# Delta-rule scan: the keys' products stored as five contiguous planes, and two moves in the first overlapped stage

## The reference

```
def step(Sm, inp):                       # one token; Sm is 8 x 8 for each head
    qi, ki, vi, bi = inp
    Sk = einsum('bhkv,bhk->bhv', Sm, ki)
    upd = ki[..., :, None] * (vi - Sk)[..., None, :]
    Sm = Sm + bi[..., None, None] * upd
    oi = einsum('bhkv,bhk->bhv', Sm, qi)
    return (Sm, oi)
...
h = hidden_states + o @ Wo
y = rmsnorm(h, ln2)
h = h + silu(y @ Wg) * (y @ Wu) @ Wd
...
h = silu(x @ w1 * s1) * (x @ w2 * s2)    # then two gelu layers 512 -> 512, and w3
```

## Time and profile before

| | |
|---|---|
| median of 3 runs | 1350.47 us (1347.79 to 1351.57) |
| profiled execution, its own time | 1351.84 us |
| its span (first to last instruction) | 1349.7 us |
| PE busy | 1164.6 us, 86% of the span |
| DVE busy | 910.4 us, 67% |
| ACT busy | 643.7 us, 48% |
| POOL busy | 473.0 us, 35% |

### The profile page before, as it was taken

The page is one execution under the profiler, slowest core; times in us unless marked ns, Lnnn a source line. Parts: engine busy times, 40 slices in busy tenths (PEclk is TensorE's granted clock), DMA queues, the critical chain, the costliest instruction groups (busy, mean ns, idle before and its releaser), DMA issues.

```text
span 1349.7 us, 19203 instructions
## 1 busy us (share of the span) xinstructions
PE 1164.6 (86%) x6118; PEld 616.3 (46%) x6118; DVE 910.4 (67%) x2097; ACT 643.7 (48%) x1258; POOL 473.0 (35%) x594
## 2 busy tenths in 40 slices
PE   5989889999898999999989581158899999999997
PEld 3434346454463554535535340124355455455553
DVE  3536535556577678686765776898888988988231
ACT  2061753745737537356365330314446745745642
POOL 3031220311323233143323136245356456466410
PEclk8989998999999999999989895578899999999999
DMA  3212030130311423314111239320220220200000
GB/s 100 83 48 71 1 110 9 46 98 34 110 41 29 139 64 81 94 33 143 39 44 42 58 70 239 97 50 9 49 58 16 58 57 16 57 24 8 24 9 8
DMA packets 85747, 79.83 MB, mean 59 GB/s; under 512 B 42800, under 2 KB 63408, under 8 KB 83632
## 3 DMA queue, kind: packets, MB, share of 16 engines
q1 hardware_dynamic: 85680, 79.01, 21.7%
HBM read 43.17 MB, written 35.00 MB: 58 GB/s over the span
## 4 chain that ended last, share of the span: by engine, by line
PE 60%; DVE 17%; ACT 10%; issue 7%; POOL 3%; DMA 2%; SPq 1%; ACTq 0%; DVEq 0%; POOLq 0%
PE ps L1318 14%; PE ps L1299 7%; PE ps L965 5%; PE ps L934 4%; PE ps L1002 4%; ACT arena L1451 4%; ACT arena L1413 3%; PE ps L968 3%; DVE arena L1850 3%; PE ps L975 3%; PE ps L1309 3%; PE ps L991 2%; PE ps L1069 2%; PE ps L1061 2%; PE ps L1051 2%
## 5 line engine op out<-in xcount | busy, mean ns | idle before, releaser
L1850 DVE TENSOR_REDUCE arena<-ps 128x4 f32<-128x512 f32 (+2 forms) x192 | 197.7, 1043 | 90.3 <-PE ps L968 87.4
L1318 PE MATMUL ps<-arena,late 128*128 128x512 f32 x512 | 227.0, 595 | 0.3 <-ACT arena L1600 0.3
L1413 ACT ACTIVATE arena<-ps 128x512 f32<-128x512 f32 (+2 forms) x200 | 109.7, 566 | 232.1 <-PE ps L934 105.6
L756 POOL TENSOR_SCALAR_AFFINE_SELECT arena<-arena 128x512 f32<-128x512 f32 x128 | 83.8, 657 | 295.1 <-ACT arena L1451 293.8
L1451 ACT ACTIVATE arena<-ps 128x1024 f32<-128x1024 f32 (+3 forms) x256 | 169.8, 711 | 33.3 <-PE ps L991 32.0
L1318 PEld LDWEIGHTS ps<-arena,late 128*128 128x128 f32 x512 | 96.3, 192 | 114.3 <-issue 112.0
L975 PE MATMUL ps<-mask_qk,ident_b 128*128 128x512 bf16 x450 | 124.2, 391 | 27.3 <-DVE arena L2134 26.1
L1600 ACT ACTIVATE arena<-ps,f_s 128x512 f32<-128x512 f32 x128 | 83.3, 688 | 109.4 <-PE ps L1318 98.5
L1413 ACT ACTIVATE arena<-ps,arena 128x128 f32<-128x128 f32 (+1 forms) x128 | 62.3, 529 | 125.1 <-DVE arena L1877 51.9
L934 PE MATMUL ps<-ident,arena 128*128 128x128 f32 (+1 forms) x624 | 99.2, 291 | 22.8 <-ACT arena L1413 13.1
L1299 PE MATMUL ps<-arena,late 128*128 128x512 f32 x256 | 115.6, 604 | 2.1 <-ACT arena L1600 2.1
(11 more groups left out here) (187 smaller groups left out, 1969.2 us busy)
## 6 DMA issues: line engine op xcount, KB each, us to landing
qr<-q_rep SPq DMA_DIRECT2D x8, 1024.0 KB, 5.6
kr<-k_rep SPq DMA_DIRECT2D x8, 1024.0 KB, 8.0
scan_d<-late SPq DMA_DIRECT2D x56, 138.0 KB, 3.0
arena<-scan_d SPq DMA_DIRECT2D x12, 552.0 KB, 6.8
q_rep<-hilo SPq DMA_DIRECT2D x24, 256.0 KB, 3.3
k_rep<-hilo SPq DMA_DIRECT2D x24, 256.0 KB, 3.9
proj_d<-arena SPq DMA_DIRECT2D x8, 768.0 KB, 5.1
late<-proj_d SPq DMA_DIRECT2D x8, 768.0 KB, 4.5
```

The costliest lines, as they stand in the source:

```text
L756: g.affine_select(out=block, in_=block, compare_op=ALU.is_ge, fill=0.0, base=0, pattern=[[0, 4], [1, P]], channel_multiplier=-1).then_inc( ...
L1318: last = pe.matmul(ps[:, ring2.bank(f"{n}{c}"), :], w[:, k, c * P:(c + 1) * P], src[:, k, :], start=(k == 0), stop=(k == HC - 1))
L1413: return act.activation(dst, src(ps[:, bank, :]), func, **kw)
L1850: v.tensor_reduce(heads[:, 2 * pr:2 * pr + 2, gs[0]:gs[-1] + 1], ps[:, at:at + 2, 0:len(gs) * w].rearrange("p q (n w) -> p q n w", w=w), X ...
```

## The change

1. `k_u` becomes five contiguous planes for each chunk, `[(chunk, j)][v][d]`: four planes of products and the old state as fifth. `live` is then a plane of 64 contiguous floats. The product writes 256 contiguous floats, reads the updates with a step of 4 floats in v (each held for 8 elements), and reads the keys with d innermost, a step of 256 bytes. The sum reads its five addends with a step of 64 floats (256 bytes), and writes 64 contiguous floats.
2. On POOL, in step 1 alone, the output products of tile 1's last quarter stand ahead of the gate products 0 and 1 of tile 0.
3. `AT_X` goes from 58 to 54: in step 1 `norm_x3` of tile 0 comes four scan instructions earlier.

```diff
-        k_u = [c2.take(QUARTER * HD, HD, CH + 1) for _ in range(2)]
-        live = [tile[:, :, :, CH].rearrange("p (c v) d -> p c v d", v=HD) for tile in k_u]
+        k_u = [c2.take(QUARTER * (CH + 1), HD, HD) for _ in range(2)]
+        live = [tile.rearrange("p (c j) v d -> p c j v d", j=CH + 1)[:, :, CH] for tile in k_u]
...
                     out_products(scan, h, 2, ahead is not None)
+                    out_products(scan, h, 3, True)
                     if ahead is not None:
                         gate_ab(ahead, 0)
                         gate_ab(ahead, 1)
-                    out_products(scan, h, 3, True)
...
-                    yield o.mark(v.tensor_tensor(k_u[half][:, rows, :, 0:CH], now_u.unsqueeze(2).broadcast_to([P, HD, HD, CH]),
-                                                 kt[:, c, :, :].unsqueeze(1).broadcast_to([P, HD, HD, CH]), ALU.mult))
+                    first = at * (CH + 1)
+                    yield o.mark(v.tensor_tensor(k_u[half][:, first:first + CH, :, :],
+                                                 now_u.rearrange("p v j -> p j v").unsqueeze(3).broadcast_to([P, CH, HD, HD]),
+                                                 kt[:, c, :, :].rearrange("p d j -> p j d").unsqueeze(2)
+                                                 .broadcast_to([P, CH, HD, HD]), ALU.mult))
...
-                    yield o.mark(v.tensor_reduce(after[:, (c + 1) % QUARTER, :, :], k_u[half][:, rows, :, :], X, ALU.add))
+                    yield o.mark(v.tensor_reduce(after[:, (c + 1) % QUARTER, :, :],
+                                                 k_u[half][:, first:first + CH + 1, :, :].rearrange("p j v d -> p v d j"), X, ALU.add))
...
-AT_Y, AT_H_FIRST, AT_H, AT_X, AT_S, AT_FIRST = 4, 21, 26, 58, 60, 44
+AT_Y, AT_H_FIRST, AT_H, AT_X, AT_S, AT_FIRST = 4, 21, 26, 54, 60, 44
```

## The result

| | median us | lowest to highest | runs |
|---|---|---|---|
| before | 1350.55 | 1345.19 to 1357.42 | 22 |
| changed | 1356.55 | 1349.88 to 1360.45 | 22 |

The ratio is 1.0041, 95% interval 1.0028 to 1.0055. Faster, at 1343.2 us, was forecast; the time lies in the stated range of 1340 to 1359, which the third rival (both far reads pay) had stretched, but on the wrong side of no change. Launches in a slower state are left out of every ratio: two of the kernel before in experiments 7 and 8, one of the changed kernel in 7, and one of 2782.51 us in experiment 6.

The account below looks back on a forecast made before the run. DVE's scan was taken to bound the start up to project_o at 953.18, PE the later steps. Terms -5.3 - 0.8 - 1.2 = -7.3 us gave 1343.2 us from 1350.47; range 1340 to 1359.

Parts of the forecast that it names:

- third rival: DVE scan: product and sum both pay fully for far reads, chunk +0.245 us, DVE becomes the bound, 1363.8 us; chance 0.27.
- Term 1: DVE's L2114: state read becomes contiguous instead of a 20-byte step, -196 ns a chunk (bounds -196 and 0).
- second rival: DVE's L2114 and ACT's L1658: state's read was not the cause, both stay slow, 1349.2 us; chance 0.06.
- Term 2: DVE's product reads keys at a 256-byte step, eight places: +20 ns a chunk (bounds 0 and +196).
- Term 3: DVE's sum reads five places 256 bytes apart: +25 ns a chunk (bounds 0 and +245).
- Term 4: ACT's copy of the states, L1658, becomes contiguous: 0.25 us off its 667 ns.
- later steps: PE's wait for ACT's takes of n2, n3 shrinks 0.25 us in five steps: -1.2 us (bounds 0 and -2.6).
- The start: From scan start to norm_x3 of tile 0: shorter chunks and AT_X bring it to 919.4 from 924.70, -5.3 us.
- GpSimd's order: Last quarter's output products ahead of the gates: 0.6 us, plus 0.2 from ACT's shorter copy, -0.8 us.
- tie: Gate product 0 comes later before layer m; the delay just fits into PE's idle 4.22 us ahead of project_o.
- The bound of 0.14 us a chunk: DVE's 2.17 us wait per step over 16 chunks: growth a chunk may take before DVE sets the step.

Follow-up runs that it names:

- experiments 7 and 8: 7: changed kernel again, 1.0026, and layout alone, 1.0058; 8: changed kernel, keys stored by token, gate product 0 ahead of output products again, 0.9965; all against before.
- experiment 6: Changed kernel with the keys of a tile stored by token, so the product reads 8 d in a row: 0.9965 to before, median 1346.28 us.
- experiment 1: Kernel before with 31 kinds of DVE instructions appended behind its last step, each twice, into scratch; single instructions timed, no kernel ratio given.
- experiments 3 and 4: Old layout: 3, GpSimd's new order plus AT_X at 54, 0.997; 4, the order alone, 0.9994, and AT_X at 54 alone, 0.9973; all against before.
- the second trace: Another trace of the unaltered changed kernel, ratio 1.0026 in that series: layer m 7.13 us, turn_h of tile 1 at 110.92 us against 110.95.
- the second series: Changed kernel timed once more beside the layout alone on one chip: 1.0026 (0.9993 to 1.006) to the kernel before.
- experiment 4's first: Kernel before with GpSimd's new order alone, AT_X at 58: 0.9994 (0.9972 to 1.0017).
- 7's first: Changed kernel run once more, unaltered, against the kernel before: 1.0026 (0.9993 to 1.006).

## Why the prediction was wrong

The step that failed is the choice between L1971 and L2114 as the nearest row for terms 2 and 3, "by the same row". Most of what stands around it held:

- **Term 1**, the state's read at -196 ns: -199. The second rival, another cause, is out (experiment 1, the held read).
- **Term 2**, the product at +20 ns: +170. **Term 3**, the sum at +25: +221. I took the 0.08 ns an element of L1971, which reads 2 or 3 places that come round, for 8 and 5 places. Experiment 1 shows the cliff just past that row, between 3 and 4 places, and nothing beyond it. A row stands for an edit only inside the range that it covers; with 3 as the most that any row had, L2114's 0.77 ns was the other end, and the two deserved even chances. The argument that the "next neighbours are wanted in the next round" was true and did not matter: 4 places whose neighbours are (591 ns) and 8 that only repeat (579 ns) both pay.
- The Trainium skill, "Advanced Engine Details and Errata", section "SBUF Cachelines", asks for at least two hits on a 16-byte line, and has a penalty where each access goes to another line. Experiment 1 agrees with the first: a step of 2 floats is free, 3 costs 70 ns for 256 elements, 4 costs 180. The second was a better guide to terms 2 and 3 than L1971, but it does not hold throughout: 2 and 3 far places taken in turn are free or nearly (287 ns for 128 elements, 372 for 192), 4 are not.
- **Term 4**, ACT's copy, 0.25 us less: 0.253. The -1.2 us that it was to give in the later steps did not show: once DVE was out of the way (experiment 6) most steps were 51.01 - 50.86 = 0.15 us shorter, not 0.25, and one longer step took that back.
- **The start.** 29.5 chunks of +0.19 and the four instructions less put `norm_x3` at 922.70 + 5.7 - 852.66 = 75.7 us from the scan's start; it came at 926.94 - 851.84 = 75.1, which is 3.1 later than before (72.0) and not 5.3 earlier. The working was right, its input wrong. `AT_X` is worth what was said, 2.1 us (experiments 3 and 4).
- **GpSimd's order**, -0.8 us with a tie behind it: `project_o` gained 0.74 on `turn_x3` in the changed kernel. The tie with the gates was sized at PE's full clock, while in this trace PE, behind its wait of 3.17 us, ran layer m at a grant of 0.70, in 10.15 us instead of 7.03. That it cost nothing by `turn_h` of tile 1 is shown by the second trace. Timed alone the order's worth can't be told from nothing (0.9994, 0.9972 to 1.0017).
- **The bound of 0.14 us a chunk** for DVE held: at +0.19 DVE set the step, at +0.02 it did not. The forecast step of the third rival's formula, 48.84 + 16 x 0.19 = 51.9, came out 0.4 us lower, at 51.47 to 51.50: DVE's busy time in a step grew by 48.64 - 45.99 = 2.65 us, not by 3.1.

What stays open: the traces account for 2.3 to 2.8 us, 0.2%, and the timed runs say 0.41% (0.28 to 0.55), in the second series 0.26% (-0.07 to 0.6). It is not the chance of one trace: the last `turn_x3` lies at 449.34 and 449.29 us in two traces of the changed kernel, and at 446.58 and 447.02 in two of the kernel before (the second is experiment 1's, whose additions stand behind it). From there to the end the first two traces agree (50.46 and 50.42 us). No run shows where the rest lies.

## What to carry to other kernels

Changing which index is innermost moved the far step from one instruction to others. So count, for each read and each write of the chain, the elements with a step of 4 floats or more and the places taken in turn, before and after. Here the old layout paid once (256 elements), the new one twice (256 + 320), and only storing a third tensor differently took one of them away. Even then the chunk was no shorter than before (2012 ns against 1989). And when an engine is nearly full in a stage that another one bounds, work out first how much it may grow; here that was 0.14 us a chunk, and the edit was past it.

## What the runs showed of the hardware

- DVE products of 4-byte elements, with one operand in PSUM: a read in SBUF with a step of 4 or 5 floats cost 0.7 ns more per element (603 and 606 ns against 421 for 256). From 4 places in turn on it cost 0.6 to 0.7 ns more: 8 places 4, 8, 16, 32 or 64 floats apart took 586, 610, 580, 579 and 579 ns (experiment 1, L2257 up to L2249). With both operands in SBUF 4 places cost the same (L2275, 589), and the sum over 5 places 691 ns, against 486 when they lie in a row (L2285). Writes with a step of 4 or 9 floats cost as much as such reads (606 and 608).
- ACT pays too: its copy of 256 elements took 667 ns at a step of 5 floats and 414 without.
- PE's granted clock was lower behind most waits of 3 to 5 us: the 16 instructions of layer m behind such a wait took 7.51 to 10.15 us in most traces, at grants of 0.70 to 0.94, and 7.03 to 7.13 in three (experiment 4's first, 7's first, 8). The same kernel with the same wait of 3.17 us had both, 10.15 and 7.13.
- The scan started between 846.07 and 858.31 us in traces of kernels that are the same up to there. The time up to the scan's start thus spreads by 12 us, and a change in part two must be read from the scan's start.
